# Two clamps of a decoder's second layer: from GpSimd's queue into VectorE's, with new queue orders

## The reference

```
x = norm(x + L0_attn(x));  x = norm(x + L0_xattn(x, ctx));  x = norm(x + L0_ffn(x))     # ffn: 8 experts, top 2
x = norm(x + L1_attn(x));  x = norm(x + L1_xattn(x, ctx));  x = norm(x + L1_ffn(x))

# L1_attn: a gated linear recurrence, 16 heads, rank 16
g = sigmoid(x @ g_w.T + g_b);  M = M * decay + (g * k * scale) outer v;  y = q . M
# L1_ffn
h = bit_linear(x, w1); h = conv1d over 3 tokens (h); h = silu(h); out = bit_linear(h, w2)
```

## The kernel before

| engine | steps and lines |
|---|---|
| TensorE | `f_x` transposes the input of the ffn (L872); `e_s` scores; `f_up` the convolution as 3 matmuls of 512 columns; `e_nm` (L844); `d_s01`, `d_s3` attention scores; `e_st`, `e_inj` the turned scores less their maximum; `d_v`, `d_out`; `e_v`, `e_out`; `d_qk`, `d_gv`, `d_rank` (all L496) |
| ScalarE | `f_x` copy (L986); `d_gates` exp (L1080); `d_sig` ln and exp (L1087, L1088); `f_exp` (L1096); `f_sig` ln and exp (L1100, L1101); `e_e0` to `e_e3` (L996); `d_v` copy (L986); `c_ln`, `d_ln`, `d_ln2`, `e_ln`, `f_ln` for the norms (L979, L980) |
| VectorE | `d_m0` to `d_m3` mask the scores (L1512); `f_norm`, `e_norm`, `c_norm` (L1222); `c_s0`, `c_s1` (L1477, L1482); `f_silu` (L1577); `f_q0` to `f_q4` quantise its output (L1554, L1558, L1562, L1581, L1585); `c_st`, `c_ag` statistics; `d_add` (L1216), `d_n0`, `d_n1` (L1523, L1528); `e_div` (L1197); `d_norm` (L1533); `d_r0`, `d_r1`, `d_rope` (L1490, L1496); `f_add` (L1591), `f_st`, `f_ag`; `f_i0` to `f_i4` quantise the ffn's input (L1554, L1558, L1562, L1569, L1573); `d_q`, `d_k` (L1500, L1506); `e_m0` to `e_m3` maxima (L1237) |
| GpSimd | `d_gate` clamp (L474); `e_res` (L470); `d_fade` (L478); `gather`, two indirect transfers (L457); `d_res`, two additions (L464, L465); `f_clamp` (L482) |

## Time and profile before

### The profile page before, as it was taken

The page is one execution under the profiler, slowest core; times in us unless marked ns, Lnnn a source line. Parts: engine busy times, 40 slices in busy tenths (PEclk is TensorE's granted clock), DMA queues, the critical chain, the costliest instruction groups (busy, mean ns, idle before and its releaser), DMA issues. The chain is left out here.

```text
span 807.0 us, 20634 instructions
## 1 busy us (share of the span) xinstructions
PE 666.1 (83%) x8166; PEld 508.4 (63%) x8166; DVE 580.3 (72%) x1607; ACT 405.3 (50%) x1172; POOL 244.9 (30%) x244
## 2 busy tenths in 40 slices
PE   5767999999999698998634958988888888988873
PEld 3355777777776476777523946766666666666641
DVE  1346888888887899886764665788777888788732
ACT  3646666666666364763210213455545455555531
POOL 5211333333333321422543132333333333333200
PEclk9959999999999799999856987999999999999965
DMA  9666534455444314540122110000000110001000
GB/s 356 235 199 208 177 129 157 155 177 172 163 157 150 137 53 158 193 164 13 29 93 72 30 30 7 9 11 12 11 13 15 15 15 11 12 12 11 5 5 7
DMA packets 48255, 72.18 MB, mean 89 GB/s; under 512 B 2832, under 2 KB 43280, under 8 KB 45472
## 3 DMA queue, kind: packets, MB, share of 16 engines
q1 hardware_dynamic: 45120, 61.80, 22.7%
q0 software_dynamic: 2320, 5.18, 3.1%
q10 hardware_dynamic: 720, 3.88, 1.2%
...
## 5 line engine op out<-in xcount | busy, mean ns | idle before, releaser
L431 POOL TENSOR_TENSOR early<-early,recb 128x616 f32<-128x616 f32 x32 | 38.8, 1214 | 212.5 <-DVE recb L1268 212.5
L957 ACT ACTIVATE sc<-sc,nmxa 128x128 f32<-128x128 f32 x256 | 78.1, 389 | 10.2 <-DVE nmxa L1182 10.2
L1512 DVE TENSOR_TENSOR k<-bank,k_sb 128x512 f32<-128x512 f32 x64 | 41.2, 686 | 35.6 <-PE bank L496 35.6
L474 POOL TENSOR_SCALAR k<-k 128x256 f32<-128x256 f32 x16 | 13.7, 858 | 158.9 <-ACT k L1080 158.9
L1178 DVE TENSOR_TENSOR sc<-bank,rel 128x512 f32<-128x512 f32 x64 | 41.1, 684 | 19.5 <-PE bank L496 19.5
L496 PE MATMUL bank<-k,xdT 128*128 128x512 f32 x96 | 49.4, 654 | 0.0
L408 POOL TENSOR_TENSOR rext<-rext,ones 128x1008 f32<-128x1008 f32 x16 | 29.9, 1867 | 60.8 <-ACT rext L942 60.8
L1190 DVE COPY pTa<-bank 128x512 f32<-128x512 f32 x32 | 21.9, 691 | 33.9 <-PE bank L548 33.9
L496 PE MATMUL bank<-pTb,v 77*32 77x128 f32 x1024 | 35.8, 284 | 9.9 <-DVE pTb L1275 4.8
L942 ACT ACTIVATE rext<-bank 128x512 f32<-128x512 f32 x64 | 34.8, 609 | 18.0 <-PE bank L496 18.0
L548 PE MATMUL bank<-k_sb,sc 128*128 128x128 f32 x256 | 37.0, 291 | 7.0 <-issue 6.1
...
## 6 DMA issues: line engine op xcount, KB each, us to landing
...
```

Source lines behind the costliest of these rows:

```text
L431: G.tensor_tensor(pB[:, part, :], pB[:, part, :], recb[:, part].unsqueeze(2).broadcast_to([P, 8, C]), ALU.mult).then_inc(b_even, 1)
L957: last = A.activation(sc[:, h, :], sc[:, h, :], ACT.Exp, bias=nmxa[:, h:h + 1])
L1512: V.tensor_tensor(scd[:, 4 * i:4 * i + 4, :], bank[(1, 2, 0, 1)[i]][:].rearrange("p (a t) -> p a t", a=4), const("causal").unsqueeze(1).br ...
```

## The change

The two clamps leave GpSimd's list and functions and become VectorE's: `f_clamp` (128x512, fp32) stands between `d_m1` and `d_m2`, `d_gate` (128x256) behind `f_norm`. All lists of `ORDER2` are written anew for it; `gather` and `d_res` on GpSimd now come ahead of `e_res` and of `d_fade` and run a tile further on against it, and `d_res(0)` gets a wait for the end of the experts' copies, whose buffer it writes into.

```diff
 ORDER2 = {
-    "dve": ("c_s0:2 c_s1:2 f_silu:-1 f_q0:-1 f_q1:-1 c_st:2 d_add:1 c_ag:2 f_q2:-1 d_st:1 f_q4:-1 d_ag:1 "
...
+    "dve": ("f_clamp:-1 d_m2:1 d_m3:1 f_silu:-1 c_s0:2 f_q0:-1 c_s1:2 c_st:2 c_ag:2 f_q1:-1 d_add:1 f_q2:-1 "
...
-    "pool": "d_gate:1 e_res d_fade:1 gather:2 d_res:1 f_clamp:-1".split(),
+    "pool": "gather:2 e_res d_res:2 d_fade:2".split(),
...
             def d_res(t):
+                if t == 0:
+                    pool.wait_ge(m_y_act, 7)
+                    pool.wait_ge(m_y_dve, 7)
                 pool.wait_ge(normed["c"], t + 1)
...
-            def d_gate_(t):
-                pool.wait_ge(d_gate0, t + 1)
-                G.tensor_scalar(eg, eg, EXP_MAX, None, ALU.min).then_inc(d_gate1, 1)
...
-            def f_clamp(t):
-                pool.wait_ge(f_e, t + 1)
-                G.tensor_scalar(he, he, EXP_MAX, None, ALU.min).then_inc(f_e1, 1)
...
+            def d_gate_(t):
+                dve.wait_ge(d_gate0, t + 1)
+                V.tensor_scalar(eg, eg, EXP_MAX, None, ALU.min).then_inc(d_gate1, 1)
+
+            def f_clamp(t):
+                dve.wait_ge(f_e, t + 1)
+                V.tensor_scalar(he, he, EXP_MAX, None, ALU.min).then_inc(f_e1, 1)
```

More of the change, by code:

```diff
@@ L85 @@
 ORDER2 = {
-    "pe": ("e_v v1:1 d_x:2 f_turn:-1 e_out d_qk:2 f_down:-1 e_x:1 d_gv:2 e_q:1 d_rank:2 f_x e_s:1 f_up e_nm:1 "
-            "d_s01:2 e_st:1 d_s3:2 e_inj:1 d_v:2 d_out:2").split(),
[3 rows of a table removed]
-            "d_k:2 d_m0:2 d_m1:2 f_norm:-1 d_m2:2 d_m3:2").split(),
-    "act": ("f_turn:-2 e_ln:-1 e_x d_gates:1 e_q f_x:-1 d_sig:1 f_exp:-1 e_nm f_ln:-2 f_sig:-1 e_e0 e_e1 e_e2 "
-            "d_v:1 e_e3 c_ln:2 d_ln:1 e_v d_x:2 d_ln2:1").split(),
-    "pool": "d_gate:1 e_res d_fade:1 gather:2 d_res:1 f_clamp:-1".split(),
+    "pe": ("v1 f_turn:-2 e_out:-1 d_qk:1 e_x d_gv:1 f_down:-2 e_q d_rank:1 f_x:-1 e_s f_up:-1 e_nm d_s01:1 "
+            "e_st d_s3:1 e_inj d_v:1 d_out:1 e_v d_x:2").split(),
[3 rows of a table added]
+            "d_gate:2 d_q:2 e_m0:1 e_m1:1 e_m2:1 e_m3:1 d_k:2 d_m0:2 d_m1:2").split(),
+    "act": ("e_e2 d_v:1 e_e3 c_ln:2 d_ln:1 e_v d_x:2 d_ln2:1 f_turn:-1 e_ln e_x:1 d_gates:2 e_q:1 f_ln:-1 f_x "
+            "d_sig:2 e_nm:1 f_exp f_sig e_e0:1 e_e1:1").split(),
+    "pool": "gather:2 e_res d_res:2 d_fade:2".split(),
     "sp": "f_store:2".split(),
@@ L489, in _ @@
             run(ORDER2["pool"], {
-                "gather": gather, "d_res": d_res, "e_res": e_res, "d_gate": d_gate_, "d_fade": d_fade,
-                "f_clamp": f_clamp}, BEGUN2)
+                "gather": gather, "d_res": d_res, "e_res": e_res, "d_fade": d_fade}, BEGUN2)
         @block.tensor
@@ L1628, in _ @@
             run(ORDER2["dve"], {
-                "c_s0": c_s0, "c_s1": c_s1, "c_norm": c_norm,
+                "c_s0": c_s0, "c_s1": c_s1, "c_norm": c_norm, "d_gate": d_gate_, "f_clamp": f_clamp,
                 "d_r0": d_turned(0), "d_r1": d_turned(1), "d_rope": d_rope_, "d_q": d_queries, "d_k": d_keys,
```

## The result

The changed kernel takes 802.65 us (median of 4 runs, 800.58 to 803.07), the kernel before, measured with it, 812.36 (4 runs, 809.8 to 813.41): a ratio of 0.9878, with a 95% interval of 0.9841 to 0.9915. A second measurement (the last group of experiments) gave 799.05 against 810.04, 0.9867 (0.9845 to 0.9889). The profiled execution took 800.58, its span is 798.8.

A forecast was written before the change was run, and what follows sets the result against it. GpSimd's ring of waits, VectorE close behind, was taken to bound rounds of 18.47 us. Start +0.7, 13 rounds -4.3, then +0.5, -0.54 and -1.04 summed to -4.7: 813.06 to 808.4 us, range 803.5 to 814.

The forecast's parts named there:

- `f_add`: VectorE, late in a round: moved behind `f_i1`, it is no longer hidden by a wait and costs +0.21 us.
- `f_i3` with `f_i4`: VectorE, just ahead of `f_x`: with GpSimd idle beside them they give 0.14 + 0.21 = 0.35 us back.
- the gate's late clamp at the start: First tile: the gate's clamp stands behind three `pass_by` products on VectorE, making `d_fade` end +1.5 us later.
- `f_x(13)` to `f_x(14)`: Third round from the end: clamp behind two masks costs 0.3, open `f_add` 0.2, together +0.5 us.
- the last two parts: Last two rounds: VectorE's clamp takes 0.48 us instead of GpSimd's 1.48, forecast as -0.54 and -1.04 us.
- the queue up to `d_add`: VectorE, mid-round: `f_sig` 0.17 us earlier, but the clamp fills 0.40 of the queue, so `d_add` only 0.04 earlier.
- rival C: VectorE's queue overlaps better, `d_add` is bound by `d_out`, 0.13 us earlier: round 18.0, time 805.7; chance 0.15.
- the odd microsecond: About 1 us more in one round before the change; may recur or not, widening all cases, outside the sum.
- the start: Up to `f_x(0)`: 1.5 us lost by the gate's clamp, 0.3 and 0.5 returned, net +0.7 us.
- The work of the two rounds behind it: Two rounds before `f_x(0)`: return 0.3 us by `c_norm` and 0.5 by `f_i3` and `f_i4`, 0.8 in all.
- `c_norm`'s gain: VectorE behind `d_add`: with `c_ag` moved ahead, `c_norm` no longer waits for `c_ln`; 0.31 us, less 0.12 for `f_q4`.
- The reason for one term: For the 0.35 us of `f_i3` and `f_i4`: GpSimd locks a shared port pair, VectorE waits out its whole instruction.

The follow-up runs named there:

- later traces: Unedited kernels profiled again: third trace of the kernel before (808.05 us, one run) against second trace of the changed kernel (799.05 us, 4 runs).
- first traces: First profiled executions of the two unedited kernels: 808.87 us for the kernel before, 800.58 us for the changed kernel.
- e9: Changed kernel plus one unused 128x512 GpSimd clamp per round, timed beside `f_i3` and `f_i4`: 801.03 us (2 runs) against 811.62.
- e10: Changed kernel plus the unused 128x512 GpSimd clamp per round, with a semaphore increment behind it: 799.64 us (one run) against 810.18.
- e1: All the new lists, but both clamps kept on GpSimd, against the kernel before: 802.19 us against 811.62, ratio 0.9895.

## Why the prediction was right and wrong

**The direction and the order of the steps held.** GpSimd left the chain, `f_sig` waits for VectorE's clamp behind two masks, VectorE then has no air up to `d_add`, `f_i3` and `f_i4` are free, `f_x` waits for `f_i4`. Of the terms, these came out as sized: `f_add` 0.20 (0.21), `f_i3` with `f_i4` 0.37 (0.35), the gate's late clamp at the start 1.4 (1.5), `f_x(13)` to `f_x(14)` +0.49 (+0.5), and in the last two parts the pieces without TensorE, -0.6 and -1.0 to -1.1 (-0.54 and -1.04). The -0.53 of the whole of `f_x(14)` to `f_x(15)` in the later traces agrees with -0.54 by luck of the pair: with either other trace of the kernel before it is -1.37 or -1.38.

**The first step that failed** is the queue up to `d_add`: "0.04 earlier, no more. Here VectorE takes back most of what GpSimd gave." It was 0.15 earlier. The clamp took 0.42 and not 0.48 and filled 0.33 of the queue (643.41 to 643.74) and not 0.40; `f_sig` came 0.24 earlier against `d_m0` and not 0.17; the masks end only 0.08 later and not 0.15. This 0.11 went through to `f_x` in full, and with the 0.02 more from `f_i3` and `f_i4` and some hundredths of rounding it makes 17.99 of 18.14. It is the round of rival C (18.0), though not for its reason: `d_add` stands at the end of a queue without gaps and not on `d_out`. Over 13 rounds this is 2.0 us.

**The second, and the larger one, is a term that was not in the sum: TensorE's clock.** The prediction saw the odd microsecond and let it "widen all cases". It should have been counted on one side, since it was paid in the rounds of the kernel before and could be lost with the change. In the first traces the clock gives 1.3 us at the start, 2.0 in two long rounds, and 0.8 and 0.7 in the TensorE pieces of the last two parts: 4.8 together. In the later traces it is 1.35 and 1.0, and nothing at the end: 2.3. That these stretches ran at the lower level before and not after is read from the traces; why the change removes them is not shown.

**The third** is the start, +0.7 for a measured -0.15 (between -0.3 and +0.1 over the traces). The loss was right. The work of the two rounds behind it returned 0.5 and not 0.8, so that without the clock the start is 1.0 to 1.4 us later and not 0.7; the 1.34 from the clock hid that.

With these the table closes in the first traces: -4.7 - 2.0 (queue) - 4.8 (clock) + 0.5 (start) + 0.3 (the round of 18.3) = -10.7, of which the later `pass_by` hides 2.5 in the span. The medians say -9.7 and -11.0.

**The sizing of `c_norm`'s gain** hides a smaller miss: 0.31 for the place of `c_ag` was 0.19 when tested alone.

**The reason for one term was wrong**, though its size was right: GpSimd holds VectorE off in parts of its instruction. Had the gate's clamp been 512 columns wide, the same overlap would have cost nothing, as e9 and e10 show.

**What the prediction did not ask** is whether the clamps had to move at all. e1 shows that with all the queues in the new orders GpSimd can keep them, and the round is as short.
